# A selective scan rebuilt in units of 1024 columns, with row-tiled matmuls and its skip term on TensorE

## What is computed

```
dbl = xc @ xproj_w.T
dtr = dbl[..., :dr]; Bs = dbl[..., dr:dr + ds]; Cs = dbl[..., dr + ds:]
dt = jax.nn.softplus(dtr @ dt_w.T + dt_b)
A = -jnp.exp(A_log)
def step(h, inp):
    dt_t, B_t, C_t, x_t = inp
    dA = jnp.exp(dt_t[..., None] * A)
    h = dA * h + (dt_t * x_t)[..., None] * B_t[:, None, :]
    y = jnp.einsum('bds,bs->bd', h, C_t)
    return (h, y)
_, ys = lax.scan(step, h0, (dt..., Bs..., Cs..., xc...))
y = ys.transpose(1, 0, 2) + xc * Dp
```

## Time and profile before

| | us |
|---|---|
| median of 3 runs | 2016.04 (2014.60 to 2017.21) |
| the profiled execution | 2014.68 |
| its span | 2012.7 |
| busy in the span: PE, DVE | 1651.0, 1585.5 |
| busy in the span: ACT, POOL | 1158.2, 1168.7 |

### The profile page before, as it was taken

One profiled execution on the slowest core, in us unless ns is written; L12 is line 12 of the kernel. 1 busy time (PEld: TensorE's weight loads), 2 busy tenths in 40 slices (PEclk: granted clock), 3 DMA queues, 4 the chain that ended last, 5 costly groups with the idle time before them and its releaser, 6 DMA issues. The chain is left out here.

```text
span 2012.7 us, 31048 instructions
## 1 busy us (share of the span) xinstructions
PE 1651.0 (82%) x9878; PEld 979.8 (49%) x9878; DVE 1585.5 (79%) x1549; ACT 1158.2 (58%) x1889; POOL 1168.7 (58%) x881
## 2 busy tenths in 40 slices
PE   5888787996788888888888888657888888888787
PEld 2555444884444454444545544234555554554333
DVE  3788745554799999999999999441899999999854
ACT  3444484334666666666666665265666665665356
POOL 0666501001467767676776775202899999999701
PEclk8999988997899999999999999777999999999898
DMA  4000000000254444444444444200000000000001
GB/s 135 2 0 0 1 0 1 1 1 1 53 95 88 90 90 87 94 83 94 89 89 83 94 91 92 44 1 0 1 1 0 0 0 0 0 0 0 7 5 42
DMA packets 23435, 78.21 MB, mean 39 GB/s; under 512 B 3792, under 2 KB 4816, under 8 KB 23120
## 3 DMA queue, kind: packets, MB, share of 16 engines
q0 software_dynamic: 18432, 67.12, 17.6%
q1 hardware_dynamic: 4944, 10.35, 1.8%
HBM read 8.25 MB, written 2.10 MB: 5 GB/s over the span
## 5 line engine op out<-in xcount | busy, mean ns | idle before, releaser
L1173 POOL TENSOR_TENSOR s_prod<-s_ahead,s_cs 128x1024 f32<-128x1024 f32 x128 | 312.2, 2439 | 203.7 <-DVE s_back L1150 103.1
L1708 POOL TENSOR_TENSOR r_prod<-r_state,r_cs 128x512 f32<-128x512 f32 x256 | 322.4, 1298 | 14.8 <-DVE r_state L1649 14.2
L1147 DVE TENSOR_TENSOR_SCAN s_ahead<-s_fore,s_pfeed 128x1024 f32<-128x1024 f32 x128 | 292.7, 2287 | 11.8 <-ACT s_fore L1069 5.3
L1150 DVE TENSOR_TENSOR_SCAN s_back<-s_aft,s_pfeed 128x1024 f32<-128x1024 f32 x128 | 289.5, 2261 | 0.0
L1069 ACT ACTIVATE s_fore<-s_pd,s_aneg 128x896 f32<-128x896 f32 x128 | 129.7, 1013 | 161.0 <-PE s_pd L940 161.0
L940 PE MATMUL s_pu<-s_partsu,selr 128*128 128x512 f32 x512 | 173.4, 462 | 52.2 <-DVE s_pfeed L1140 52.0
L1636 DVE TENSOR_TENSOR r_feed<-r_pu,r_bs 128x512 f32<-128x512 f32 x256 | 164.4, 687 | 61.9 <-PE r_pu L1478 61.9
L1140 DVE TENSOR_TENSOR s_pfeed<-s_pu,s_bs 128x1024 f32<-128x1024 f32 x128 | 157.8, 1233 | 37.7 <-PE s_pu L940 25.0
L1601 ACT ACTIVATE r_decay<-r_pd,r_aneg 128x512 f32<-128x512 f32 x256 | 168.3, 686 | 23.2 <-PE r_pd L1478 23.0
L1478 PE MATMUL r_pu<-r_parts,selr 128*128 128x512 f32 x512 | 161.3, 437 | 5.7 <-DVE r_feed L1636 5.7
L1649 DVE TENSOR_TENSOR_SCAN r_state<-r_decay,r_carry,r_feed 128x512 f32<-128x512 f32 x128 | 156.3, 1263 | 0.0
(11 more groups left out here) (255 smaller groups left out, 3338.1 us busy)
## 6 DMA issues: line engine op xcount, KB each, us to landing
s_ahead<-s_back POOLq DMA_DIRECT2D x128, 512.0 KB, 4.5
x_act<-in_x_dram SPq DMA_DIRECT2D x8, 256.0 KB, 5.4
out_dram<-x_act SPq DMA_DIRECT2D x16, 128.0 KB, 2.3
k_scan<-in_pack_scan_dram SPq DMA_DIRECT2D x1, 1600.0 KB, 10.4
k_fir<-in_pack_fir_dram SPq DMA_DIRECT2D x1, 1600.0 KB, 13.8
k_l<-in_pack_l_dram SPq DMA_DIRECT2D x1, 450.0 KB, 6.9
k_ln<-in_pack_ln_dram SPq DMA_DIRECT2D x3, 131.0 KB, 3.0
k_mlp<-in_pack_mlp_dram SPq DMA_DIRECT2D x2, 194.0 KB, 5.1
```

The lines of the kernel that those rows point to most:

```text
L1147: dve.tensor_tensor_scan(ahead[:, v % 4], f, feed[:], 0.0, ALU.mult, ALU.add).then_inc(ahead_done, 1)
L1150: dve.tensor_tensor_scan(back[:, v % 4, ::-1], a[:, ::-1], feed[:, ::-1], 0.0, ALU.mult, ALU.add).then_inc(back_done, 1)
L1173: pool.tensor_tensor(prod[:, b], ahead[:, v % 4], cs[:, buf].rearrange("p i n -> p (i n)"), ALU.mult).then_inc(prod_done, 1)
L1708: pool.tensor_tensor(prod[:, v % 2, q], state[:, v % 2, q], cs[:, v % UNROLL // 4, q], ALU.mult).then_inc(multiplied, 1)
```

## The change

The diff rewrites `scan3` and adds its loop, `skewed3`. A unit is now one quarter, one g and the 1024 columns of a whole image, 128 units; the scan always starts from 0 and `carry` is gone. Two chunks (`half`) must be split before a unit can start. Units alternate between two quarters (`phase` picks which two). r_pu and r_pd are one tile of two banks each, and so is `feed`.

Per unit, TensorE makes r_pu of unit s-16 and r_pd of unit s-15 together, eight matmuls with 32 rows each (`tile_position=(32 * q, 0)`), in turn for the two; the quarters of the two always differ. VectorE has one feed and one scan of 1024 columns. The product with C is written over `state`, which has four slots. y is summed for two units at a time. The skip term is a matmul with `place`, 128 x 4 x 128 numbers which VectorE scales with Dp once, and which also sorts two chunks into r_py; ScalarE copies r_py out in two pieces of 64 partitions. The rest of bc is made by a matmul with minus the identity (`negid`) on top of r_pm and copied by ScalarE; `one` minus 1 is ScalarE's too. The pack of constants `l3` grows by 5 x 128 columns.

The diff, cut to its core:

```diff
+UNROLL3, PEEL3 = 32, 32
+
+
+def skewed3(eng, body):
+
+
+
+    for s in range(PEEL3):
+        body(s, s)
+    with eng.Fori(0, (UNITS - PEEL3) // UNROLL3) as r:
+        for u in range(UNROLL3):
+            body(r * UNROLL3 + (PEEL3 + u), u)
+    for s in range(UNITS, UNITS + PEEL3):
+        body(s, s % UNROLL3)
...
-        state, prod = m.sb("r_state", [P, 2, Q4, N]), m.sb("r_prod", [P, 2, Q4, N])
-        carry = m.sb("r_carry", [P, Q4, Q4])
...
-        ps_d, ps_u, feed = m.banks("r_pd", 2), m.banks("r_pu", 2), m.banks("r_feed", 2)
...
+        wdt, place, negid = m.sb("r_wdtb", [P, P]), m.sb("r_place", [P, 4, P]), m.sb("r_negid", [P, P], F32R)
...
+        parts_d, parts_u, parts_bc = (m.sb("r_parts" + t, [P, 2, 2, 2 * N], F32R) for t in ("d", "u", "bc"))
+        decay, state = (m.sb("r_" + t, [P, 4, 2 * N]) for t in ("decay", "state"))
+        bs, cs = (m.sb("r_" + t, [P, 2, 2, 2 * N]) for t in ("bs", "cs"))
+        ps_d, ps_u, feed = (m.banks("r_p" + t, 1, (P, 2 * N))[0] for t in ("d", "u", "feed"))
...
-        LAG_B, LAG_D, LAG_U, LAG_Y = 2, 5, 6, 7
-        DT, DU, BC = range(3)
+        LAG_B, LAG_E, LAG_D, LAG_A, LAG_P, LAG_Y, LAG_V = 11, 15, 16, 17, 18, 19, 20
...
+        def cells(u):
+
+            u %= UNROLL3
+            half, phase = u // 16, u % 16 // 8
+            return half, phase, 2 * phase + u % 2, u % 8 // 2
...
+                k, par, gi = u % 8, u // 16, s - u % 8
+                if k == 2 and live(s, UNITS):
+                    at = slice(u % 16 // 8 * N, (u % 16 // 8 + 1) * N)
+                    pe.wait_ge(hi_bc, gi + 8)
+                    pe.matmul(ps_m[:], negid[:], parts_bc[:, par, 0, at], start=False, stop=True,
+                              skip_group_check=True).then_inc(bc_rest, 8)
...
+                jobs = []
+                if live(p, UNITS):
+                    half, _, q, g = cells(u - LAG_D)
+                    if (u - LAG_D) % 16 == 0:
+                        pe.wait_ge(lo_u, p + 16)
+                    wait(pe, fed, p)
+                    jobs.append((ps_u, parts_u[:, half], q, g))
+                if live(e, UNITS):
+                    half, _, q, g = cells(u - LAG_E)
+                    if (u - LAG_E) % 16 == 0:
+                        pe.wait_ge(lo_d, e + 16)
+                    wait(pe, decayed, e)
+                    jobs.append((ps_d, parts_d[:, half], q, g))
+                for chunk in range(2):
+                    for part in range(2):
+                        for bank, parts, q, g in jobs:
+                            rows, at = slice(32 * q, 32 * q + 32), slice(chunk * N, (chunk + 1) * N)
+                            mm = pe.matmul(bank[:, at], selr[rows, (4 * q + g) * P:(4 * q + g + 1) * P],
+                                           parts[rows, part, at], start=(part == 0), stop=(part == 1),
+                                           tile_position=(32 * q, 0))
+                            if chunk == 1 and part == 1:
+                                mm.then_inc(u_rep if bank is ps_u else d_ps, 1)
...
+                    wait(pe, s_copied, w)
+                    if k == 1 and live(s, UNITS):
+                        pe.wait_ge(relu_done, gi + 8)
+                    if k == 2 and live(s, UNITS):
+                        pe.wait_ge(lo_bc, gi + 8)
+                    sel = 16 + 2 * q + which
+                    for part in range(2):
+                        mm = pe.matmul(ps_m[:], selr[rows, sel * P:(sel + 1) * P], parts_bc[rows, half, part, at],
+                                       start=(part == 0), stop=(part == 1), tile_position=(32 * q, 0))
+                    mm.then_inc(s_rep, 1)
...
+                o, z = s - LAG_Y, (u - LAG_Y) % UNROLL3
+                if z % 2 == 1 and live(o, UNITS):
+                    _, phase, _, g = cells(z)
+                    if z % 8 == 1:
+                        wait(pe, y_done, o - 1)
+                        for chunk in range(2):
+                            pe.matmul(ps_y[:], place[:, 2 * phase + chunk],
+                                      xc[:, columns(o - z % 16 + 8 * chunk, N)], start=(chunk == 0), stop=False,
+                                      skip_group_check=True)
+                    pe.wait_ge(multiplied, o + 1)
+                    for chunk in range(2):
+                        for q in (2 * phase, 2 * phase + 1):
+                            quad = (q + 2 * chunk) % 4
+                            mm = pe.matmul(ps_y[quad * 32:(quad + 1) * 32], ysel[:, g * 32:(g + 1) * 32],
+                                           state[:, (z - 1 + q % 2) % 4, chunk * N:(chunk + 1) * N], start=False,
+                                           stop=(g == 3), tile_position=(0, quad * 32), skip_group_check=True)
+                    mm.then_inc(y_part, 2)
...
+                if k < 2 and live(s, UNITS):
+                    if live(w, UNITS):
+                        pe.wait_ge(s_copied, w + 1)
+                    if k == 0:
+                        wait(pe, lo_bc, gi)
+                        pe.matmul(ps_m[:], wdt[:], xc[:, columns(gi, N)], start=True, stop=True).then_inc(dt_ps, 8)
...
+                        pe.wait_ge(relu_done, gi + 8)
+                        pe.matmul(ps_m[:], c["wbc"], xc[:, columns(gi, N)], start=True, stop=True).then_inc(bc_ps, 8)
+
+            skewed3(pe, body)
...
+                o, z = s - LAG_V, (u - LAG_V) % UNROLL3
+                if z % 8 == 7 and live(o, UNITS):
+                    phase = z % 16 // 8
+                    act.wait_ge(y_part, o + 1)
+                    for chunk in range(2):
+                        rows, src = slice(phase * 64, phase * 64 + 64), (phase + chunk) % 2 * 64
+                        done = act.activation(xc[rows, columns(o - z % 16 + 8 * chunk, N)], ps_y[src:src + 64],
+                                              ACT.Copy)
+                    done.then_inc(y_done, 8)
+                if k == 2 and live(s, UNITS):
+                    act.wait_ge(bc_rest, gi + 8)
+                    act.activation(parts_bc[:, par, 1, at], ps_m[:], ACT.Copy).then_inc(lo_bc, 8)
...
+                    wait(act, scanned, e - 3)
+                    act.activation(decay[:, v % 4], ps_d[:], ACT.Exp, scale=aneg[:, g:g + 1]).then_inc(decayed, 1)
...
+                    act.activation(ex[:], ps_m[:], ACT.Abs, bias=c["dtb"]).then_inc(away_done, 8)
...
+                    act.activation(delta[:], ps_m[:], ACT.Relu, bias=c["dtb"]).then_inc(relu_done, 8)
+                    act.wait_ge(away_done, gi + 8)
+                    act.activation(ex[:], ex[:], ACT.Exp, scale=-1.0).then_inc(ex_done, 8)
+                if k == 1:
+                    act.wait_ge(bc_ps, gi + 8)
+                    wait(act, s_rep, gm - 16)
+                    act.activation(parts_bc[:, par, 0, at], ps_m[:], ACT.Copy).then_inc(hi_bc, 8)
+                    act.wait_ge(ex_done, gi + 8)
+                    act.activation(one[:], ex[:], ACT.Copy, bias=1.0).then_inc(one_done, 8)
+                if k == 2:
+                    act.wait_ge(one_done, gi + 8)
+                    act.activation(ln[:], one[:], ACT.Ln).then_inc(ln_done, 8)
+                    act.wait_ge(ln_done, gi + 8)
+                    act.activation(one[:], one[:], ACT.Copy, bias=-1.0).then_inc(grown_done, 8)
...
+            dve.tensor_scalar(place[:].rearrange("p a b -> p (a b)"), c["place"], c["dp"], None,
+                              ALU.mult).then_inc(ready, 1)
+            dve.tensor_copy(negid[:], c["negid"]).then_inc(ready, 1)
...
-                if live(p, STEPS):
-                    b, g, lc = v % 2, v % 4, v % UNROLL // 4
-                    def inflow(q):
-                        dve.wait_ge(u_rep, 4 * p + q + 1)
-                        if g == 0:
-                            dve.wait_ge(b_copied, p + q + 1)
-                        wait(dve, scanned, 4 * p + q - 1)
-                        dve.tensor_tensor(feed[q % 2][:], ps_u[q % 2][:], bs[:, lc, q], ALU.mult).then_inc(fed, 1)
-
...
-                    inflow(0)
-                    inflow(1)
-                    scan(0)
-                    scan(1)
-                    inflow(2)
-                    inflow(3)
-                    scan(2)
-                    scan(3)
...
+                p, v = s - LAG_A, u - LAG_A
+                if live(p, UNITS):
+                    _, phase, q, _ = cells(v)
+                    dve.wait_ge(u_rep, p + 1)
+                    if v % 8 < 2:
+                        dve.wait_ge(s_copied, p + 2 + v % 8)
+                    wait(dve, scanned, p)
+                    dve.tensor_tensor(feed[:], ps_u[:], bs[:, phase, q % 2], ALU.mult).then_inc(fed, 1)
+                    dve.wait_ge(fed, p + 1)
+                    dve.wait_ge(decayed, p + 1)
+                    wait(dve, y_part, p - 3)
+                    dve.tensor_tensor_scan(state[:, v % 4], decay[:, v % 4], feed[:], 0.0, ALU.mult,
+                                           ALU.add).then_inc(scanned, 1)
...
```

(18 more changed lines are left out.)

286 lines of the change are left out of this document (80 added, 206 removed).

## The result

The changed kernel takes 2167.53 us, the median of four runs (2163.80 to 2169.22), against 2015.86 of the kernel before (2014.60 to 2017.21) beside it: ratio 1.0753, 95% interval 1.0737 to 1.0769. The forecast of slower was right, its size was not: 2034 was predicted, 2076 was the upper end.

The account below looks back on a forecast made before the run. GpSimd and VectorE were taken to share the bound. Floor 469.8 + stalls 21.0 + 13.6 = 504.4 us against 491.1: +13.3; ends +4.4; +17.7 in all, so 2034 us as a median, range 2003 to 2076.

Parts of the forecast that it names:

- The forecast of slower: Sign for the whole kernel: slower than before, given chance 0.70, against 0.22 faster and 0.08 same.
- Part 1: VectorE's pace in the third scan: 128 units of 3.67 us make a floor of 469.8 us, against 491.1 before.
- Part 2: GpSimd in the third scan: 28.2 us a chunk against VectorE's 29.4, lateness covered, so nothing added.
- Part 3: TensorE's r_pu and r_pd: row tiles overlap, a pair costs 0.23 us, a tile-kind change 0.1 us a step.
- The two rules of the Trainium skill: TensorE tiling prices not used in the sum: pair 0.30 us, giving 2043; drain 0.27 us, giving 2040.
- the case that was summed to 2034: Whole kernel with overlapping row tiles and the summed stalls: 2022 to 2046 us, chance 0.52.
- Part 4: Chain dt, bc, negid through bank r_pm: r_pu behind negid stalls VectorE 1.5 us in 14 chunks, 21.0 us.
- rival B: TensorE's row tiles don't overlap, stalls of 14 x 3.3 + 16 x 1.8: 2074 us (2060 to 2085), chance 0.18.
- my walk: Step-by-step timing of TensorE's and ScalarE's queue from a feed's start: r_pu ready at 12.4 us, wanted at 11.0.
- Part 5: Skip term: place matmuls (1.98 us a pair) ahead of y make a scan wait 0.85 us in 16 chunks, 13.6 us.
- Part 6: The third scan's ends: +2 us before the first feed, +1.4 after the last scan, +1 for loading constants.
- Rival C: TensorE's lateness before r_pu and y fits into the slack: faster, 1999 us, or 2011 with a third of stalls; chance 0.21.

Follow-up runs that it names:

- everything else was mended: Changed kernel with full-row selector matmuls, r_pu first, two r_pu tiles, place moved, negid and that step's B or C later: 2025.51 us.
- full rows: Changed kernel with every selector matmul (r_pu, r_pd, B or C) over all 128 rows, one after another: 2085.07 us.
- the best version: The 2025.51 us kernel (full-row selector matmuls and all four edits) with the copies of B and C one step sooner: 2014.88 us.

## Why the prediction was right in sign and wrong in size

**Part 1 held**: 3.66 us a unit for 3.67, scans 2287 ns, feeds 1233.

**Part 2 held for the bound**: GpSimd is busy 309.34 us of 480, a product lasts 2363 ns for the bound of 2.52. "I add nothing" lacked a term: GpSimd waits for the last copy of C (100.4 us of the 480 in the changed kernel), and once everything else was mended a step's head start there was worth 10.6 us (2025.51 to 2014.88). What it costs in the changed kernel itself, at the low clock, no run shows.

**Part 3 is the step that failed.** The overlap was forecast rightly (pairs at 0.23 us, once the clock is up). The price of a change of tile kind was taken as 0.1 us a step; measured are 0.08 in a step without y and 0.18 in one with y. The two rules of the Trainium skill that stood beside it gave more for the pair and the change than the rows do: the trace has two row tiles at once for the time of one, where the Trainium skill (TensorE: Matmul & The Clock Gate, section Part 3: Packing small matmuls) has 3.07 for four. Three at once, as at 1727.46, keep that pace; no run here has four. And the Trainium skill's "drains" (TensorEngine Tiling (Array Packing), section Key Properties) is here 0.08 to 0.10 us, not the 0.27 that I estimated from it. What failed is under all of that: each TensorE duration of Parts 3 to 5 was taken from rows of before, where the clock is 0.98, and put to work in a stage where it is 0.59. At that level the pair costs 0.43, y 1.94 for 1.06, dt 2.08 for 1.12. No rival had the clock in it. Taking the row tiles back is worth 82.5 us of the 133.5 that the forecast was short by. This isn't the price of the clock alone, since the same edit gives up the overlap and saves changes of tile kind. What the kernel would take with overlapping tiles at the full clock, the case that was summed to 2034, no run shows, so the stalls of 1.5 and 0.85 us were never seen by themselves, and that the forecast of slower came true doesn't prove them.

**Part 4**: mechanism and place were right, and so, at the full clock, nearly was the size. At full rows, which is rival B's case, my walk gave 0.6, 2.4 and 0.3 us a chunk. In the 14 chunks of that run's 480 us the stall behind negid is 2.28 to 2.46 us ten times and 3.46 to 3.91 four times; the two beside it are mostly 0.8 to 0.9 and 0.6. Here is one of the four:

```profile
1633.13 1.23 DVE L1672 TENSOR_TENSOR r_pfeed<-r_pu,r_bs 128x1024 f32<-128x1024 f32 x1 [0.91 <-PE r_pu L1527]
...
1640.69 1.23 DVE L1672 TENSOR_TENSOR r_pfeed<-r_pu,r_bs 128x1024 f32<-128x1024 f32 x1 [3.91 <-PE r_pu L1527]
1642.52 2.29 DVE L1676 TENSOR_TENSOR_SCAN r_state<-r_decay,r_pfeed 128x1024 f32<-128x1024 f32 x1 [0.60 <-PE r_py L1564]
```

```profile
1637.49 0.63 PE L1527 MATMUL r_pu<-r_partsu,selr 128*128 128x512 f32 x1
...
1640.05 0.60 PE L1527 MATMUL r_pu<-r_partsu,selr 128*128 128x512 f32 x1
```

From the first r_pu to the end of the last pass 3.16 us, where a step at the full clock has 1.90: though the mean clock of this run is 0.99, TensorE is at 1.2 GHz behind negid in these four chunks. It had idled 1.35 us ahead of bc and 0.91 ahead of negid, but it idled 1.32 and 0.83 in the chunk before, where r_pu and r_pd follow at 0.23 us and the stall is 2.43. So these waits alone don't decide it, and what does isn't shown. B's 2074 with its upper end of 2085 met 2085.07 at that end.

**Part 5** was nearly exact: 16 x 1.8 = 29 us for the serial case, 26.4 measured. In the changed kernel itself the stall is 3.51 us instead of 0.85. From r_pu's start (1720.58) to the end of y (1726.30 + 1.23) pass 6.95 us where the walk had 4.5: place takes 1.8 of the difference, r_pu, r_pd and B or C 0.6, y 0.1.

**Part 6** held for the two ends: 34.1 us from first dt (1381.19) to first feed for 33.5, 5.7 us behind the last scan for 5.6. The constants' load takes 1.1 us more, for +1, against the earlier trace rows; whether anything waited for it wasn't tested:

```profile
k_l<-in_pack_l_dram SPq DMA_DIRECT2D x1, 515.0 KB, 3.5
```

**Rival C**, the chains fitting into the slack, is what the later runs build on purpose. It decides as the prediction said, by what stands ahead of r_pu, but y in the same queue decides with it: two edits that brought r_pu forward and not y gave 0.9 and 8.9 us, and one that brought y forward at the cost of r_pu lost 14.4. Of the 15.0 us of waits for y that are left in the best version, 11.5 are 13 stalls of 0.7 to 1.1 us in the steps with negid. One of them, with ScalarE's copy, bc, y and the scan:

```profile
1666.14 0.59 ACT L1627 ACTIVATE r_cs<-r_pm 128x512 f32<-128x512 f32 x1
...
1666.83 1.10 PE L1585 MATMUL r_pm<-y_inner,k_l 128*128 x2 [1.27 <-issue]
...
1669.93 1.06 PE L1570 MATMUL r_py<-r_state,ysel 128*32 128x512 f32 x8
...
1671.16 2.29 DVE L1685 TENSOR_TENSOR_SCAN r_state<-r_decay,r_pu 128x1024 f32<-128x1024 f32 x1 [1.04 <-PE r_py L1570]
```

GpSimd's products were done by 1667.64, so y isn't late for them. It stands in TensorE's queue behind bc, r_pu, r_pd and negid, and bc starts when ScalarE's copy has left r_pm, after 1.27 us in which TensorE idles. That is Part 4's bank again. It is read from the trace: no run gives that version a second bank, or takes work off TensorE.

## What to carry to other kernels

When an edit changes how much of TensorE's array a matmul uses, the granted clock belongs among the rivals, with every TensorE duration in the sum taken at both levels, and one small run (the old order, the new tiles) prices it alone. When VectorE waits for two results of one in-order queue, ask for each edit which of the two it moves: a gain on one that leaves the other is none. And before a scan's or a product's operand is moved from PSUM to SBUF, ask what GpSimd reads at that time.

## What was not expected of the hardware

**Few rows, low clock.** One order of work, three widths: 0.98, 0.86 and 0.57 for 128, 64 and 32 rows, with TensorE busy 85 to 91% of the stretch in all three. A matmul of 32 rows costs the same 0.23 us at the full clock as one of 128.

**VectorE and GpSimd take turns.** With the feed in SBUF a scan has two inputs there. GpSimd's rows, then VectorE's, of that run:

```profile
1703.30 2.35 POOL L1693 TENSOR_TENSOR r_state<-r_state,r_cs 128x1024 f32<-128x1024 f32 x1
1705.61 3.26 POOL L1710 TENSOR_TENSOR r_du<-r_delta,y_inner 128x512 f32<-128x512 f32 x1
```

```profile
1703.64 4.15 DVE L1677 TENSOR_TENSOR_SCAN r_state<-r_decay,r_feed 128x1024 f32<-128x1024 f32 x1
```

The product holds until 1705.65. The scan, issued at 1703.64, ends 2.3 us after about 1705.5, its own length. du, issued at 1705.61, ends 1.1 us after the scan, where it takes 1.27 alone. Each waits for the whole of the other rather than both going slower. The Trainium skill (SBUF — State Buffer, section Who interferes with whom) calls it "an exclusive lock"; the trace agrees, with scans of 2290 to 4526 ns. With the feed in PSUM every scan takes 2.29 us beside the same GpSimd work.
